# Selective-scan layer: the sums of two states' products made by accumulating DMAs, and added to y two slots later

## The chip, the core and the metric

The program runs on one core of one Trainium2 chip. The metric is the device time of the whole program in microseconds. The kernel before took 4594.26 us, the median of three runs (4590.93, 4594.26 and 4594.27). One more execution was recorded by the profiler; all rows below are from that one. Its first to its last instruction span 4588.9 us.

## The reference, cut to what matters

Input x has 4 sequences of 4096 positions with 512 features. A modulated layer norm is followed by a selective scan over 16 states, a gate and an output projection, then a second modulated norm and a small feed-forward part. The part that matters here is the scan and the sum over its states:

```
def step(h, inp):
    xt, dtt, bt, ct = inp
    dA = jnp.exp(A[None] * dtt[..., None])
    dB = dtt[..., None] * bt[:, None, :]
    h = dA * h + dB * xt[..., None]
    y = jnp.sum(h * ct[:, None, :], axis=-1)
    return (h, y)
...
y = y + D[None, None, :] * x_ssm
y = y * z
y = y @ w_out.T + b_out
```

Everything is float32. For each feature and position there are 16 products h * C, one for each state, and y is their sum.

## The kernel before, in words

**Chunks and units.** The 4 x 4096 positions are cut into 32 chunks of 512. Features lie on the 128 partitions in KD = 4 blocks. A unit is one state n of one block j: a tile of 128 partitions by 512 positions. A chunk has U = 64 units, numbered i = 4 n + j. The program is one long software pipeline: while chunk s is scanned, the projections of the next chunk f = s + 1 are made, and the output of chunk b = s - 1 and the feed-forward part of chunk c = s - 2 are finished. Each engine has its own loop over the 64 slots of a step and runs its instructions strictly in the order written; the table `ORDER` sets at which slot each piece of dense work stands.

**One unit on its way.** ScalarE makes the decay (L829) and dt * x * B (L839). TensorE transposes the latter into one of two banks of `b_ps` (`turn_v`, L453), four 128 x 128 transposes to a unit. VectorE scans (L1127) from that bank and the decay into one of 6 places of `hs`. GpSimd, called POOL in the profile, multiplies by the broadcast C row (`product`, L364) into one of PR_RING = 9 places of `pr`. TensorE adds the product to `y_ps` by four accumulating transposes (`add_unit`, L530).

**Held states.** For the states in HELD = (0, 6, 8, 13) TensorE adds nothing. When the product of the next state (1, 7, 9, 14; `summed`) is there, POOL adds the held product, which lies four units back, to it (`add_products`, L375), and TensorE adds that sum alone. So TensorE transposes 48 units of a chunk instead of 64, and POOL makes 16 sums. A unit's `add_unit` stands LAG = 4 slots after it; near the end of a chunk some stand earlier, and the last three fall in the first two slots of the next step.

**What else stands in POOL's row.** After the product (and the sum) of a slot, POOL does what is due there: the skip term (L369, slots 8 to 11), the step size dt of the next chunk for block m (`step_size`: dt by L402 at slots 42, 45, 48, 51 and u = dt * x by L410 one slot later), the gate of the present chunk (`gate`, L415) with its last block at slot 6 of the next step, and the residual additions (L384, L389).

**Who waits for POOL.** `turn_u` on TensorE transposes u of the next chunk (`dense<-ident,xn`, a L453 row; u lies in the memory of `xn`). Its first call stands in slot 54 and waits until all four blocks of u are there (`u_done` equal to KD), that is for the L410 of slot 52. `take_y` on VectorE multiplies the gate into y (L1165); its fourth block waits for the last gate, and the first `add_out` on TensorE (L566, slot 9) waits for that. `turn_v` for unit i + 1 waits for the scan of unit i - 1.

Of the kernel before, what the change touches and what calls it, by code (L numbers as in the profile page):

```python
def build_program(nc, ap, B, L, D, N, M, INNER):
# [5 lines left out]
    ALU = mybir.AluOpType  # L7
# [16 lines left out]

    HELD = (0, 6, 8, 13)
    RELU_RING = 3


# [35 lines left out]
    def summed(n):  # L64
        return n - 1 in HELD

    def sums(i):

        return sum(summed(r // KD) for r in range(i + 1))

    def added(i):

        return sum(r // KD not in HELD for r in range(i + 1))

    def slot(*part):
        return int(BEGIN[".".join(str(n) for n in part)] * U / TOTAL)
# [8 lines left out]
    with ctx:  # L85
# [15 lines left out]
        ident = sb("ident", [P, P])  # L101
# [48 lines left out]
        pr = work[:, at_pr:].rearrange("p (r t) -> p r t", r=PR_RING)  # L150
# [15 lines left out]
        def inside(s, *group):  # L166
# [8 lines left out]

        PER = {
            "SP": dict(stored_0=Q, stored_1=Q, stored_2=Q, stored_3=Q, c_stored=Q),
            "Pool": dict(prod_done=U, skip_added=KD, sum_done=sums(U - 1), xsh_done=TB, x1_done=TB, dt_done=KD, u_done=KD, sz_done=KD),
            "PE": dict(b_made=U, y_added=added(U - 1), s_ps=1, g_used=J, yz_ps=KD, out_ps=TB, res_used=TB, pre_ps=TB, xt_ps=KD, xs_ps=KD,
                       cb_ps=1, bt_ps=1, x2_ps=KD, dt_ps=KD, z_ps=KD, ut_ps=TB),  # L180
            "ACT": dict(dec_done=U, v_done=N * TB, rel_done=J, gm_done=1, lnp_done=TB, rstdp_done=TB,
                        lnx_done=1, rstdx_done=1, ln2_done=1, rstd2_done=1, t2_done=TB, xn_done=TB,
# [9 lines left out]
        x_loaded, xb_loaded, c_loaded, wm_loaded = (  # L192
            [ctx.enter_context(nc.semaphore(f"{n}_{m}")) for m in range(count)]
            for n, count in (("x_loaded", TB), ("xb_loaded", TB), ("c_loaded", C_RING), ("wm_loaded", 6)))

        def at(name, k, n):

            return (k + FIRST) * COUNT[name] + n if k < NCH else (NCH + FIRST) * COUNT[name]

        def count_up(eng, name):  # L200
            for n, c in PER[name].items():
# [138 lines left out]
        def _(gp):  # L340
# [13 lines left out]
            def product(s, i):  # L354
                n, j = i // KD, i % KD
                if j == 0:
                    gp.wait_ge(c_loaded[(s * N + n) % C_RING], ((s * N + n) // C_RING + 1) * Q)
                gp.wait_ge(S["scan_done"], at("scan_done", s, i + 1))
                k, r = (s, i - PR_RING) if i >= PR_RING else (s - 1, U + i - PR_RING)
                if r // KD in HELD:  # L360
                    gp.wait_ge(S["sum_done"], at("sum_done", k, sums(r + KD)))
                else:
                    gp.wait_ge(S["y_added"], at("y_added", k, added(r)))
                gp.tensor_tensor(pr[:, (s * U + i) % PR_RING, :], hs[:, (s * U + i) % HS_RING, :],  # L364
                                 c_bc[:, (s * N + n) % C_RING, :], ALU.mult).then_inc(S["prod_done"], 1)
                if i in SKIP_AT:
                    gp.wait_ge(S["prod_done"], at("prod_done", s, i + 1))
                    gp.wait_ge(S["skip_done"], at("skip_done", s, j + 1))
                    gp.tensor_tensor(pr[:, (s * U + i) % PR_RING, :], pr[:, (s * U + i) % PR_RING, :],  # L369
                                     xs_t[:, j, :], ALU.add).then_inc(S["skip_added"], 1)  # L370

            def add_products(s, i):

                gp.wait_ge(S["prod_done"], at("prod_done", s, i + 1))
                gp.tensor_tensor(pr[:, (s * U + i) % PR_RING, :], pr[:, (s * U + i) % PR_RING, :],  # L375
                                 pr[:, (s * U + i - KD) % PR_RING, :], ALU.add).then_inc(S["sum_done"], 1)

            def attended(b):
                for tb in range(TB):
# [68 lines left out]
        def _(pe):  # L448
# [68 lines left out]

            def add_unit(s, i):
                j = i % KD
                if i // KD in HELD:  # L520
                    return
                if i == KD:
                    pe.wait_ge(S["y_copied"], at("y_copied", s - 1, TB))
                if summed(i // KD):
                    pe.wait_ge(S["sum_done"], at("sum_done", s, sums(i)))
                pe.wait_ge(S["prod_done"], at("prod_done", s, i + 1))
                if i in SKIP_AT:
                    pe.wait_ge(S["skip_added"], at("skip_added", s, j + 1))
                for tb in range(TB):
                    last = mm(y_ps[:, tb, j * P:(j + 1) * P], pr[:, (s * U + i) % PR_RING, tb * P:(tb + 1) * P],  # L530
                              ident[:, :], is_transpose=True, start=(i == KD), stop=(i == U - 1))
                last.then_inc(S["y_added"], 1)

            def add_g(s, c, k):
# [258 lines left out]
            def step(s, has_s, has_f, has_b, has_c):  # L793
                f, b = s + 1, s - 1
                chains = [dense(s, has_s, has_f, has_b, has_c)]
                if s == 0:
                    chains.insert(0, late_rows())
                beside = Beside(*chains)
                for i in range(U):
                    if has_s and i + 1 < U:  # L800
                        turn_v(s, i + 1)
                    beside.until(i)
                    if has_f and i + 1 == U:
                        turn_v(f, 0)
                    if has_b and i < 2:
                        for r in ((U - 3, U - 2), (U - 1,))[i]:
                            add_unit(b, r)
                    if has_s and i >= LAG + 1:
                        for r in {LAG + 1: (0, 1), LAG + 2: (2,), U - 1: (U - 5, U - 4)}.get(i, (i - LAG,)):
                            add_unit(s, r)  # L810

            steps(step)
# [210 lines left out]
        def _(dve):  # L1023
# [129 lines left out]
            def take_y(s, b, c):  # L1153
                for tb in range(TB):
                    yield 2 + tb // 2
                    dve.wait_ge(S["dec_done"], at("dec_done", b, U))
                    dve.wait_ge(S["u_done"], at("u_done", b, KD))
                    dve.wait_ge(S["y_added"], at("y_added", b, added(U - 1)))
# [160 lines left out]
```

## Time and profile before

| | before |
|---|---|
| median of 3 runs | 4594.26 us |
| span of the profiled execution | 4588.9 us |
| runs' median over that span | 5.4 us |
| TensorE (PE) busy | 4344.2 us, 95% |
| POOL busy | 4161.1 us, 91% |
| ScalarE (ACT) busy | 3817.6 us, 83% |
| VectorE (DVE) busy | 3679.8 us, 80% |
| POOL: 2048 products (L364) | 2590.8 us |
| POOL: 512 sums (L375) | 653.4 us |
| granted TensorE clock, mean | 0.991 |

The profile has no time for the profiled execution but its span; the runs' median is 5.4 us longer than that, which is what lies ahead of the first and after the last instruction. Busy time is time in which an engine executes; a TensorE that is busy need not be at its peak, since matmuls overlap and their ends are modelled. How far TensorE is ahead or behind is better read from where a group of matmuls starts and where the next one does.

### The profile page before, as it was taken

What the parts mean: (1) busy time and instruction counts of PE and PEld (TensorE: products, weight loads), DVE (VectorE), ACT (ScalarE), POOL (GpSimd) and SP (SyncE); (2) the same over time, 40 slices, a digit from 0 to 9 for tenths busy, and PEclk for the clock granted to TensorE, in tenths of its full rate; (3) what the DMA queues carried; (4) which work ended last, traced back from release to release, by engine and by line L of the source; (5) the groups of instructions that cost most, each with busy time, mean ns of one, the idle gap of its engine ahead of it and who ended that gap; (6) DMA issues with size and microseconds to landing.
All of it is one profiled execution on the core that took longest, in us unless ns stands there. A gap on an engine that the chain in (4) does not pass through costs nothing. (4 is left out here: it accounts for less than half of the span.)

```text
span 4588.9 us, 71982 instructions
## 1 busy us (share of the span) xinstructions
PE 4344.2 (95%) x22528; PEld 2805.6 (61%) x22528; DVE 3679.8 (80%) x5132; ACT 3817.6 (83%) x6371; POOL 4161.1 (91%) x3343
## 2 busy tenths in 40 slices
PE   7999999999999999999999999999999999999997
PEld 3666666666666666666666666666666666666664
DVE  3778888888887888888888888888878888888885
ACT  3788888888888888888888888888888888888885
POOL 3899999999999999999999999999999999999995
PEclk8999999999999999999999999999999999999999
DMA  3111111111111111111121111111111111111111
GB/s 129 45 43 58 58 58 45 56 51 57 60 58 48 49 59 59 58 46 54 51 62 59 59 44 56 51 57 60 54 45 54 60 61 58 47 53 51 58 49 39
DMA packets 140915, 254.79 MB, mean 56 GB/s; under 512 B 18597, under 2 KB 18597, under 8 KB 140538
## 3 DMA queue, kind: packets, MB, share of 16 engines
q1 hardware_dynamic: 140538, 250.19, 17.2%
q8 instruction: 184, 3.01, 0.3%
q14 instruction: 193, 1.58, 0.1%
HBM read 215.50 MB, written 34.63 MB: 55 GB/s over the span
## 5 line engine op out<-in xcount | busy, mean ns | idle before, releaser
L364 POOL TENSOR_TENSOR work<-work,c_bc 128x512 f32<-128x512 f32 x2048 | 2590.8, 1280 | 266.6 <-DVE work L1127 180.9
L1127 DVE TENSOR_TENSOR_SCAN work<-work,state,b_ps 128x512 f32<-128x512 f32 x1792 | 2250.5, 1273 | 351.9 <-PE b_ps L453 343.2
L839 ACT ACTIVATE work<-u_td,b_td 128x512 f32<-128x512 f32 x2048 | 1455.4, 711 | 147.5 <-PE b_ps L453 142.2
L829 ACT ACTIVATE work<-dt_t,neg_a 128x512 f32<-128x512 f32 x2048 | 1454.1, 710 | 12.5 <-DVE work L1127 12.1
L453 PE MATMUL b_ps<-ident,work 128*128 128x128 f32 x8192 | 1246.2, 275 | 67.2 <-DVE work L1127 57.0
L453 PEld LDWEIGHTS b_ps<-ident,work 128*128 128x128 f32 x8192 | 966.7, 142 | 344.5 <-issue 173.4
L530 PEld LDWEIGHTS y_ps<-ident,work 128*128 128x128 f32 x6144 | 758.4, 142 | 635.7 <-issue 586.5
L530 PE MATMUL y_ps<-ident,work 128*128 128x128 f32 x6144 | 916.2, 274 | 4.7 <-POOL work L375 3.5
L375 POOL TENSOR_TENSOR work<-work 128x512 f32<-128x512 f32 x512 | 653.4, 1276 | 40.2
L679 PE MATMUL dense<-h_t,w_in_t 128*128 128x512 f32 x1024 | 514.4, 599 | 9.2 <-DVE u_td L1210 8.9
L587 PE MATMUL dense<-w_out_t,proj 128*128 128x512 f32 x1024 | 508.6, 594 | 0.0
L645 PE MATMUL dense<-xs_t,w_dt_t 128*128 128x512 f32 x1024 | 501.2, 593 | 0.0
L616 PE MATMUL dense<-h_t,w_in_t 128*128 128x512 f32 x1024 | 497.9, 595 | 1.0 <-ACT h_t L843 1.0
L1127 DVE TENSOR_TENSOR_SCAN work<-work,b_ps 128x512 f32<-128x512 f32 x256 | 306.5, 1213 | 65.7 <-PE b_ps L453 61.8
L453 PE MATMUL dense<-ident,xn 128*128 128x128 f32 x1536 | 243.6, 283 | 76.3 <-ACT xn L899 36.9
L453 PEld LDWEIGHTS dense<-ident,xn 128*128 128x128 f32 x1536 | 181.2, 144 | 207.2 <-issue 80.8
L539 PE MATMUL dense<-tmp,w_dg 128*128 128x512 f32 x512 | 245.4, 593 | 1.8 <-ACT tmp L861 1.8
L679 PEld LDWEIGHTS dense<-h_t,w_in_t 128*128 128x128 f32 x1024 | 166.7, 190 | 111.5 <-issue 76.0
L861 ACT ACTIVATE tmp<-gm,b,w 128x512 f32<-128x512 f32 x256 | 201.7, 801 | 37.4 <-PE dense L539 24.8
L616 PEld LDWEIGHTS dense<-h_t,w_in_t 128*128 128x128 f32 x1024 | 168.4, 191 | 82.6 <-issue 82.6
L402 POOL TENSOR_TENSOR dt_t<-dt_t,tmp 128x512 f32<-128x512 f32 x128 | 163.7, 1279 | 52.0 <-ACT tmp L971 52.0
L645 PEld LDWEIGHTS dense<-xs_t,w_dt_t 128*128 128x128 f32 x1024 | 165.5, 191 | 66.9 <-issue 66.9
(115 smaller groups left out, 4523.0 us busy)
## 6 DMA issues: line engine op xcount, KB each, us to landing
c_bc<-c_d SPq DMA_DIRECT2D x512, 256.0 KB, 3.2
xn<-in_x SPq DMA_DIRECT2D x128, 256.0 KB, 5.1
x<-in_x SPq DMA_DIRECT2D x128, 256.0 KB, 4.4
out_dram<-x SPq DMA_DIRECT2D x128, 256.0 KB, 4.2
work<-in_wmod SPq DMA_DIRECT2D x2, 1024.0 KB, 6.3
w_in_t<-in_w_in_t SPq DMA_DIRECT2D x2, 1024.0 KB, 9.9
gain_shift<-par_d SPq DMA_DIRECT2D x8, 256.0 KB, 4.5
w_dt_t<-in_w_dt_t SPq DMA_DIRECT2D x1, 1024.0 KB, 11.3
```

The lines of the kernel that those rows point to most:

```text
L364: gp.tensor_tensor(pr[:, (s * U + i) % PR_RING, :], hs[:, (s * U + i) % HS_RING, :], c_bc[:, (s * N + n) % C_RING, :], ALU.mult).then_inc( ...
L375: gp.tensor_tensor(pr[:, (s * U + i) % PR_RING, :], pr[:, (s * U + i) % PR_RING, :], pr[:, (s * U + i - KD) % PR_RING, :], ALU.add).then_i ...
L453: return nc.tensor.transpose(dst, src, ident[:, :])
L530: last = mm(y_ps[:, tb, j * P:(j + 1) * P], pr[:, (s * U + i) % PR_RING, tb * P:(tb + 1) * P], ident[:, :], is_transpose=True, start=(i == ...
L539: mm(long(s, "g")[:, :], w2_dg[:, k, :], tmp[:, k % RELU_RING, :], start=(k == 0), stop=(k == J - 1)).then_inc(S["g_used"], 1)
L587: last = mm(long(s, "pre", tb)[:, :], yz_t[:, k, tb * P:(tb + 1) * P], w_out[:, k, :], start=False, stop=(k == KD - 1))
L616: last = mm(long(s, "xs", m)[:, :], w_in[:, k, m * P:(m + 1) * P], h_t[:, f % 2, k, :], start=(k == 0), stop=(k == KD - 1))
L645: last = mm(long(s, "dt", m)[:, :], w_dt[:, k, m * P:(m + 1) * P], xs_t[:, k, :], start=(k == 0), stop=(k == KD - 1))
L679: last = mm(long(s, "z", m)[:, :], w_in[:, k, D + m * P:D + (m + 1) * P], h_t[:, s % 2, k, :], start=(k == 0), stop=(k == KD - 1))
L829: A(decay[:, (s * U + i) % DEC_RING, :], dt_t[:, s % 2, j, :], ACT.Exp, scale=neg_a[:, j, n:n + 1]).then_inc(S["dec_done"], 1)
L839: A(v[:, n % V_RING, tb, :], u_td[:, tb, :], ACT.Copy, scale=b_td[:, s % 2, tb, n:n + 1]).then_inc(S["v_done"], 1)
L1127: V.tensor_tensor_scan(hs[:, (s * U + i) % HS_RING, :], decay[:, (s * U + i) % DEC_RING, :], b_ps[:, i % 2, :], state[:, i:i + 1] if s % N ...
```

## The change

The sum of a held product and the next one is no longer a POOL instruction: POOL issues a DMA that adds the held unit's tile to the other's, both in on-chip memory, one DMA for each unit (16 to a chunk). Each block j has a semaphore of its own, `sum_done[j]`, which the DMA raises by Q = 16 when it has landed. `add_unit` of a summed unit stands SUM_LAG = 2 slots later than before, six slots after its unit. The fourth held state is 11 instead of 13, so that the last four sums are made in slots 48 to 51 instead of 56 to 59. `ADDS` lists the 48 units that TensorE adds in the order of their slots; the accumulation starts and ends with its first and last one. At the end of a chunk units 61, 62 and 63 are all added in slot 1 of the next step, where 61 and 62 were in slot 0.

```
-    HELD = (0, 6, 8, 13)
+    HELD = (0, 6, 8, 11)
+    SUM_LAG = 2
...
+    def add_slot(r):
+
+        return r + LAG + SUM_LAG * summed(r // KD) - (r in (U - 4, U - 2, U - 1)) - (r == U - 1)
+
+    ADDS = sorted((r for r in range(U) if r // KD not in HELD), key=lambda r: (add_slot(r), r))
...
                 if r // KD in HELD:
-                    gp.wait_ge(S["sum_done"], at("sum_done", k, sums(r + KD)))
+                    if k >= 0:
+                        gp.wait_ge(sum_done[r % KD], k * SUMS + Q * sums(r + KD))
...
             def add_products(s, i):
 
                 gp.wait_ge(S["prod_done"], at("prod_done", s, i + 1))
-                gp.tensor_tensor(pr[:, (s * U + i) % PR_RING, :], pr[:, (s * U + i) % PR_RING, :],
-                                 pr[:, (s * U + i - KD) % PR_RING, :], ALU.add).then_inc(S["sum_done"], 1)
+                gp.dma_start(pr[:, (s * U + i) % PR_RING, :], pr[:, (s * U + i - KD) % PR_RING, :],
+                             accum_op=ALU.add).then_inc(sum_done[i % KD], Q)
...
                 if summed(i // KD):
-                    pe.wait_ge(S["sum_done"], at("sum_done", s, sums(i)))
+                    pe.wait_ge(sum_done[j], s * SUMS + Q * sums(i))
...
-                    if has_b and i < 2:
-                        for r in ((U - 3, U - 2), (U - 1,))[i]:
+                    for r in ADDS:
+                        if has_b and add_slot(r) == U + i:
                             add_unit(b, r)
-                    if has_s and i >= LAG + 1:
-                        for r in {LAG + 1: (0, 1), LAG + 2: (2,), U - 1: (U - 5, U - 4)}.get(i, (i - LAG,)):
+                    for r in ADDS:
+                        if has_s and add_slot(r) == i:
                             add_unit(s, r)
```

Line numbers of the changed kernel are 8 to 10 higher at these places: the product L364 is L374 there, the sum L375 is the DMA L385, L402 and L410 are L412 and L420, and on TensorE L453, L530, L660 and L679 are L463, L538, L668 and L687.

On POOL, slots 47 to 52 of a step before: products (L364) with dt (L402) and u (L410) of the next chunk, blocks 2 and 3, between them.

```order
L364 TENSOR_TENSOR work<-work,c_bc 128x512 x2
L402 TENSOR_TENSOR dt_t<-dt_t,tmp 128x512
L364 TENSOR_TENSOR work<-work,c_bc 128x512
L410 TENSOR_TENSOR xn<-dt_t,xs_t 128x512
L364 TENSOR_TENSOR work<-work,c_bc 128x512 x2
L402 TENSOR_TENSOR dt_t<-dt_t,tmp 128x512
L364 TENSOR_TENSOR work<-work,c_bc 128x512
L410 TENSOR_TENSOR xn<-dt_t,xs_t 128x512
```

The same place of the changed kernel, from the first of the four sums, that of unit 48:

```order
L385 DMA work<-work 128x512
L412 TENSOR_TENSOR dt_t<-dt_t,tmp 128x512
L374 TENSOR_TENSOR work<-work,c_bc 128x512
L385 DMA work<-work 128x512
L420 TENSOR_TENSOR xn<-dt_t,xs_t 128x512
L374 TENSOR_TENSOR work<-work,c_bc 128x512
L385 DMA work<-work 128x512
L374 TENSOR_TENSOR work<-work,c_bc 128x512
L385 DMA work<-work 128x512
L412 TENSOR_TENSOR dt_t<-dt_t,tmp 128x512
L374 TENSOR_TENSOR work<-work,c_bc 128x512
L420 TENSOR_TENSOR xn<-dt_t,xs_t 128x512
```

Four DMA issues now stand among these rows, all of them ahead of the L420 that completes u.

On TensorE, slots 51 to 54 before: a unit's transpose (`b_ps`), one or two z projections (L679), the addition to y (L530), and in slot 54 the first transpose of u (`dense<-ident,xn`).

```order
L453 MATMUL b_ps<-ident,work 128x128 x4
L679 MATMUL dense<-h_t,w_in_t 128x512
L530 MATMUL y_ps<-ident,work 128x128 x4
L453 MATMUL b_ps<-ident,work 128x128 x4
L660 MATMUL dense<-ident,cb_t 128x32 x4
L679 MATMUL dense<-h_t,w_in_t 128x512
L530 MATMUL y_ps<-ident,work 128x128 x4
L453 MATMUL b_ps<-ident,work 128x128 x4
L679 MATMUL dense<-h_t,w_in_t 128x512 x2
L530 MATMUL y_ps<-ident,work 128x128 x4
L453 MATMUL b_ps<-ident,work 128x128 x4
L453 MATMUL dense<-ident,xn 128x128 x4
```

The changed kernel from slot 52 to slot 55:

```order
L463 MATMUL b_ps<-ident,work 128x128 x4
L668 MATMUL dense<-ident,cb_t 128x32 x4
L687 MATMUL dense<-h_t,w_in_t 128x512
L463 MATMUL b_ps<-ident,work 128x128 x4
L687 MATMUL dense<-h_t,w_in_t 128x512 x2
L463 MATMUL b_ps<-ident,work 128x128 x4
L463 MATMUL dense<-ident,xn 128x128 x4
L538 MATMUL y_ps<-ident,work 128x128 x4
L463 MATMUL b_ps<-ident,work 128x128 x4
L687 MATMUL dense<-h_t,w_in_t 128x512 x2
L538 MATMUL y_ps<-ident,work 128x128 x4
```

The additions to y that stood in slots 48 to 53 are gone from there (six groups of four), so the transpose of u comes earlier by as much; the six stand in slots 56 to 59, which had none.

## Rows read from the trace of the kernel before

**Rows 1.** The page's head and busy time of each engine

```profile
span 4588.9 us, 71982 instructions
PE 4344.2 (95%) x22528; PEld 2805.6 (61%) x22528; DVE 3679.8 (80%) x5132; ACT 3817.6 (83%) x6371; POOL 4161.1 (91%) x3343
```

**Rows 2.** Costliest groups: line, engine, operation, count | busy, mean ns | idle before

```profile
L364 POOL TENSOR_TENSOR work<-work,c_bc 128x512 f32<-128x512 f32 x2048 | 2590.8, 1280 | 266.6 <-DVE work L1127 180.9
...
L375 POOL TENSOR_TENSOR work<-work 128x512 f32<-128x512 f32 x512 | 653.4, 1276 | 40.2
```

**Rows 3.** Waits, all engines: who waited for whom, us in total, times, longest

```profile
DVE proj L1165 <- POOL sz_t L415: 64.5, 30, 2.3
...
PE dense L566 <- DVE proj L1165: 45.2, 30, 1.5
```

**Rows 4.** Waits of TensorE alone

```profile
PE dense L453 <- POOL xn L410: 5.6, 6, 2.8
```

**Rows 5.** Busy time in slots 48 to 53 of one step, 13.55 us long

```profile
core 0: us, PE busy (x) PEld busy (x) DVE busy (x) ACT busy (x) POOL busy (x), PEclk, DMA share, GB/s
2274.35:2287.90 13.55, 13.55 (x73) 8.75 (x72) 8.62 (x11) 9.27 (x16) 13.55 (x12) 1.00 0.14 41
```

**Rows 6.** TensorE in order of time: start, length, group [idle before, releaser]

```profile
2287.45 0.60 PE L530 MATMUL y_ps<-ident,work 128*128 128x128 f32 x4
2287.89 0.60 PE L453 MATMUL b_ps<-ident,work 128*128 128x128 f32 x4
2288.41 0.63 PE L453 MATMUL dense<-ident,xn 128*128 128x128 f32 x4
2288.87 0.60 PE L530 MATMUL y_ps<-ident,work 128*128 128x128 f32 x4
2289.60 0.63 PE L453 MATMUL b_ps<-ident,work 128*128 128x128 f32 x4
...
2296.53 0.66 PE L453 MATMUL dense<-ident,xn 128*128 128x128 f32 x4 [0.65 <-DVE tmp L1225]
...
2301.36 1.13 PE L679 MATMUL dense<-h_t,w_in_t 128*128 128x512 f32 x2 [0.29 <-DVE u_td L1210]
```

**Rows 7.** POOL in order of time, the same step, slots 46 to 53

```profile
2272.85 1.27 POOL L364 TENSOR_TENSOR work<-work,c_bc 128x512 f32<-128x512 f32 x1
2274.08 1.29 POOL L410 TENSOR_TENSOR xn<-dt_t,xs_t 128x512 f32<-128x512 f32 x1
2275.32 2.51 POOL L364 TENSOR_TENSOR work<-work,c_bc 128x512 f32<-128x512 f32 x2
2277.79 1.26 POOL L402 TENSOR_TENSOR dt_t<-dt_t,tmp 128x512 f32<-128x512 f32 x1
...
2286.42 1.26 POOL L410 TENSOR_TENSOR xn<-dt_t,xs_t 128x512 f32<-128x512 f32 x1
```

**Rows 8.** VectorE in order of time: the scan of unit 46

```profile
2270.31 1.27 DVE L1127 TENSOR_TENSOR_SCAN work<-work,state,b_ps 128x512 f32<-128x512 f32 x1
```

**Rows 9.** POOL in order of time at the start of that step, slots 4 to 6

```profile
2177.61 1.28 POOL L364 TENSOR_TENSOR work<-work,c_bc 128x512 f32<-128x512 f32 x1 [2.08 <-DVE work L1127]
2180.03 1.28 POOL L364 TENSOR_TENSOR work<-work,c_bc 128x512 f32<-128x512 f32 x1 [1.14 <-issue]
2181.38 1.28 POOL L375 TENSOR_TENSOR work<-work 128x512 f32<-128x512 f32 x1
2182.62 1.29 POOL L364 TENSOR_TENSOR work<-work,c_bc 128x512 f32<-128x512 f32 x1
...
2187.82 1.27 POOL L415 TENSOR_TENSOR sz_t<-sz_t,tmp 128x512 f32<-128x512 f32 x1
```

**Rows 10.** VectorE at the same place

```profile
2189.22 0.69 DVE L1165 TENSOR_TENSOR proj<-sz_t,dense 128x512 f32<-128x512 f32 x1 [2.13 <-POOL sz_t L415]
```

**Rows 11.** TensorE at the same place

```profile
2187.52 0.60 PE L530 MATMUL y_ps<-ident,work 128*128 128x128 f32 x4
...
2190.06 1.10 PE L566 MATMUL dense<-wout_g,gm 128*128 128x512 f32 x2 [1.50 <-DVE proj L1165]
...
2194.06 0.60 PE L530 MATMUL y_ps<-ident,work 128*128 128x128 f32 x4
```

**Rows 12.** SyncE's issues of the C rows' DMAs, 256 KB each: duration ns min/median/max

```profile
L298 SPq DMA_DIRECT2D c_bc<-c_d x512: 319/320/430, 65.0 to 4502.0; - x171
...
DMA to landing us min/median/max: 3.0/3.2/4.8
```

**Rows 13.** DMA issues by line: KB each, median us from issue to landing

```profile
xn<-in_x SPq DMA_DIRECT2D x128, 256.0 KB, 5.1
```

More of the change, by code:

```diff
@@ L67, in sums, with added @@
     def sums(i):
-        return sum(summed(r // KD) for r in range(i + 1))
-    def added(i):
-        return sum(r // KD not in HELD for r in range(i + 1))
+        return sum(summed(n) for n in range(i // KD + 1))
+    def add_slot(r):
+        return r + LAG + SUM_LAG * summed(r // KD) - (r in (U - 4, U - 2, U - 1)) - (r == U - 1)
+    ADDS = sorted((r for r in range(U) if r // KD not in HELD), key=lambda r: (add_slot(r), r))
+    def added(r):
+        return ADDS.index(r) + 1
     def slot(*part):
@@ L177, in build_program @@
             "SP": dict(stored_0=Q, stored_1=Q, stored_2=Q, stored_3=Q, c_stored=Q),
-            "Pool": dict(prod_done=U, skip_added=KD, sum_done=sums(U - 1), xsh_done=TB, x1_done=TB, dt_done=KD, u_done=KD, sz_done=KD),
-            "PE": dict(b_made=U, y_added=added(U - 1), s_ps=1, g_used=J, yz_ps=KD, out_ps=TB, res_used=TB, pre_ps=TB, xt_ps=KD, xs_ps=KD,
+            "Pool": dict(prod_done=U, skip_added=KD, xsh_done=TB, x1_done=TB, dt_done=KD, u_done=KD, sz_done=KD),
+            "PE": dict(b_made=U, y_added=len(ADDS), s_ps=1, g_used=J, yz_ps=KD, out_ps=TB, res_used=TB, pre_ps=TB, xt_ps=KD, xs_ps=KD,
                        cb_ps=1, bt_ps=1, x2_ps=KD, dt_ps=KD, z_ps=KD, ut_ps=TB),
@@ L191, in build_program @@
         S = {n: ctx.enter_context(nc.semaphore(n)) for n in once + list(COUNT)}
-        x_loaded, xb_loaded, c_loaded, wm_loaded = (
+        x_loaded, xb_loaded, c_loaded, wm_loaded, sum_done = (
             [ctx.enter_context(nc.semaphore(f"{n}_{m}")) for m in range(count)]
-            for n, count in (("x_loaded", TB), ("xb_loaded", TB), ("c_loaded", C_RING), ("wm_loaded", 6)))
+            for n, count in (("x_loaded", TB), ("xb_loaded", TB), ("c_loaded", C_RING), ("wm_loaded", 6), ("sum_done", KD)))
         def at(name, k, n):
             return (k + FIRST) * COUNT[name] + n if k < NCH else (NCH + FIRST) * COUNT[name]
+        SUMS = Q * len(HELD)
         def count_up(eng, name):
@@ L519, in add_unit @@
                 j = i % KD
-                if i // KD in HELD:
-                    return
-                if i == KD:
+                if i == ADDS[0]:
                     pe.wait_ge(S["y_copied"], at("y_copied", s - 1, TB))
                 if summed(i // KD):
-                    pe.wait_ge(S["sum_done"], at("sum_done", s, sums(i)))
+                    pe.wait_ge(sum_done[j], s * SUMS + Q * sums(i))
                 pe.wait_ge(S["prod_done"], at("prod_done", s, i + 1))
@@ L530, in add_unit @@
                     last = mm(y_ps[:, tb, j * P:(j + 1) * P], pr[:, (s * U + i) % PR_RING, tb * P:(tb + 1) * P],
-                              ident[:, :], is_transpose=True, start=(i == KD), stop=(i == U - 1))
+                              ident[:, :], is_transpose=True, start=(i == ADDS[0]), stop=(i == ADDS[-1]))
                 last.then_inc(S["y_added"], 1)
@@ L1157, in take_y @@
                     dve.wait_ge(S["u_done"], at("u_done", b, KD))
-                    dve.wait_ge(S["y_added"], at("y_added", b, added(U - 1)))
+                    dve.wait_ge(S["y_added"], at("y_added", b, len(ADDS)))
                     V.tensor_copy(y_sb[:, b % 2, tb, :], y_ps[:, tb, :]).then_inc(S["y_copied"], 1)
```

## The prediction

> **What bounds the kernel now.** I read the page's busy times first. TensorE is busy 95% of the span and POOL 91%, the others 80 to 83% [rows 1], so either of two engines may set the pace. The groups show what the change takes off POOL: 512 sums of 1.276 us, 653 us in all [rows 2]. Read as a share, that is a seventh of the span; the question is what of it stands on the path.
>
> The second view is the busy time of one stretch. In slots 48 to 53 TensorE and POOL are both busy for the whole 13.55 us at a granted clock of 1.00, while VectorE has 8.62 us of work [rows 5]. In order of time TensorE's groups there follow each other at their issue distance, 0.44 us for four transposes (2287.45 to 2287.89) [rows 6]. So in the second half of a step TensorE sets the pace, and POOL is only just not late: its backlog of products does no harm as long as no TensorE instruction needs its end.
>
> The third view, the waits, says where POOL does reach the others. VectorE waits 64.5 us in 30 steps for the last gate, and TensorE's L566 45.2 us in 30 for VectorE right behind it [rows 3]: about 1.5 us a step at its start. And TensorE has waited for u (L410) 6 times, 5.6 us in all [rows 4]. That row is small, but it shows that the second contact exists and has little slack. The two places decide this change.
>
> **The start of a step.** In the step shown POOL makes product 4 at 2180.03, its sum, product 5 at 2182.62, two more sums, and the gate at 2187.82 [rows 9]. VectorE stands 2.13 us until the gate is there [rows 10], and TensorE's L566 starts at 2190.06 after 1.50 us of waiting for VectorE [rows 11]. A summed product takes 2.59 us from start to start (2180.03 to 2182.62), an unsummed one 1.24 (2274.08 to 2275.32) [rows 7, 9]; so a sum costs POOL 1.35 us, 0.07 of it waiting for its own product. A DMA that occupies POOL for d would cost d + 0.07, and three of them stand ahead of the gate: it comes 3 x (1.28 - d) earlier. At most about 2 us of that is of use: VectorE waits no longer than 2.13, and TensorE, which loses an addition to y in slot 8 (0.44 us, the one at 2187.52), would stand 1.50 + 0.44. The additions of slots 8 and 9 come back in slots 12 and 13. There they fill waits that I count as unchanged.
>
> **The end of a step, where the cost is.** Two edits meet here. Six additions leave slots 48 to 53, so TensorE reaches the first transpose of u not at 2288.41 but 6 x 0.44 = 2.64 us earlier, at 2285.77 [rows 6]. VectorE can follow that pace: 8.62 us of work in the 10.9 that are left [rows 5]. Meanwhile four sums enter POOL's row between product 48 and the last L410, a stretch in which POOL had no gap. Before, that stretch ran from 2276.56 (the second of the two products that start at 2275.32) to 2287.68 (2286.42 + 1.26), 11.12 us [rows 7]. With four DMAs it takes 11.12 + 4 x (d + 0.07).
>
> It may begin earlier. The eight sums in slots 28 to 39 save 8 x (1.28 - d), 2.2 us for d = 1, but product 46 can't start ahead of its scan's end at 2271.58 [rows 8] (2270.31 + 1.27); at 2271.66 it would be 1.19 us earlier than it was, 2272.85, and product 48 follows three steps of 1.24 later, at 2275.38. Then u is complete at 2275.38 + 11.12 + 0.28 + 4d = 2286.78 + 4d. TensorE is there at 2285.77 and waits 1.0 + 4d. It executes strictly in order, so behind that wait stand the next units' transposes, and VectorE's scans behind those. The six additions left out are still owed in slots 56 to 59, so none of the wait is got back by them; they only fill the waits that follow: 0.29 us before the b_ps group at 2289.60 (2288.87 + 0.44 = 2289.31), 0.65 at 2296.53 and 0.29 at 2301.36 [rows 6], together 1.23. VectorE, which has done two scans more by then, is no later. The end of a step gets longer by 4d - 0.2.
>
> **What d is.** No row shows a DMA issued by POOL. The nearest below is SyncE's issue of a DMA of the same 256 KB, 0.32 us [rows 12]; less than that isn't to be expected of an instruction that must give out the same 128 rows. The nearest on POOL is its own pass over 128 rows, 1.28 us [rows 2]. The far end above is that POOL stands until the data has landed, 3.2 to 5.1 us [rows 12, 13]. POOL has to work out the transfer itself, so I take a value nearer to POOL's row than to SyncE's, three quarters of the way from 0.32 to 1.28: 1.0 us.
>
> The Trainium skill, DMA: Bandwidth & Descriptors, section Latency and other measured facts, gives about 1 us to the first byte for a DMA that GpSimd issues, against 600 ns from the others, and lays it to the GpSimd cores writing the descriptors. Taken as d, an estimate, it gives the same sum; no row here shows it. The same page, section Anatomy of one DMA, calls descriptor generation small and gives most of the delay to the landing; by that d would be near the lower end, the first rival below.
>
> **The sum.** For d = 1.0: the end of a step costs 1.0 + 4.0 - 1.23 = 3.8 us, its start gives back 3 x 0.28 = 0.84: 3.0 us a step. 31 steps have both places, 92 us. The profiled execution's span is 4588.9; 5.4 us lie around it by the runs' median of 4594.3. So 4594.3 + 92 = 4686.
>
> **Edits that I cost at nothing.** The later additions and the landing: the sum of unit 4, issued at about 2181.4, is added where unit 6 was, at 2194.06 [rows 9, 11], 12.7 us later; a 256 KB transfer lands in 3.2 to 5.1 us [rows 12, 13]. The ring: product i + 5 reuses the place of the unit that was added to product i; four products and the issue, 4 x 1.24 + d = 6 us, lie between. If landing took longer than that, POOL would stand for the difference. TensorE's work is the same 48 units. Units 61 and 62 moved from slot 0 to slot 1: unit 63's place, for which the copies of y wait, is the same. SyncE issues what it did. The transfers (512 of 256 KB, 134 MB) meet queues that are seldom full; if not, they land later, which is the third rival.
>
> **Rivals.**
> *Cheap issue: faster.* If POOL only hands the DMA on, d = 0.32 as on SyncE, the end of a step costs 4 x 0.32 - 0.2 = 1.1 and the start gives its full 2.0: -0.9 a step, 29 us, 4565. For it speaks that a DMA moves no data through POOL; against it that on POOL's row every listed operation of this width costs 1.28. The point of decision is d = 0.58, where 4d - 0.2 equals 3 x (1.28 - d).
> *Issue as long as the sum or longer.* At d = 1.28 nothing is saved: the gate comes when it did, product 46 is not earlier (1.19), and the end costs 1.0 + 1.19 + 5.1 - 1.23 = 6.1 us a step: 4783. Each further 0.1 us adds over 1 us a step. For it: every transfer of this kind names three rows (two read, one written); against: nothing in the trace.
> *Late landing.* An addition reads its target as well; at twice 5.1 us the ring's 6 us are overrun by 4, in slots 35 to 40, where POOL has some slack, and TensorE stands for sums four times a step: some 6 us a step on top, 4870. Against: the queues' light load.
> *The wait for u doesn't form,* because TensorE doesn't get ahead, or POOL runs earlier than I count: then only the start counts, 0.84 to 2 us a step, 4568 to 4532.
>
> **How the numbers follow.** My forecast, d from 0.75 to 1.1, has 0.36 and by itself spans 4631 (1.2 us a step) to 4707 (3.6). Cheap issue has 0.24, no wait 0.06, d around 0.58 with less than 9 us either way 0.12, an issue of over 1.1 us 0.18, late landing 0.04. A change under 0.2% (9 us) can't be told from none. So faster 0.30, same 0.12, slower 0.58. The range, 4560 to 4785, leaves out the larger gains below and the long issues and late landings above.
>
> **What would show it.** The profile after should have DMA issues on POOL of about 1 us (the first thing to read); TensorE's transpose of u waiting for POOL's L420 in some 31 steps, about 5 us each; the wait for the gate shorter by less than 1 us; POOL's busy time, without its issues, down by 653 us, and the span longer all the same. It is wrong if issues take under 0.6 us or if the wait for u stays a rare one.

## The result: 4.9% slower, and the profile after

The changed kernel takes 4815.9 us (median of 4 runs, 4815.3 to 4816.9), the kernel before on the same chip 4592.9: ratio 1.0486, 95% interval 1.0471 to 1.0501. That is 223 us, 7.0 us in each of the 32 steps. The forecast was 4686 within 4560 to 4785. The sign is right, the size is more than twice the forecast and outside the range.

The page of the kernel after, the head and three of its groups (line, engine, operation, count | busy, mean ns | idle before), answers to [rows 1, 2]:

```profile
span 4813.9 us, 71981 instructions
...
PE 4412.0 (92%) x22528; PEld 2866.4 (60%) x22528; DVE 3677.8 (76%) x5132; ACT 3822.5 (79%) x6371; POOL 3989.7 (83%) x3343
...
L374 POOL TENSOR_TENSOR work<-work,c_bc 128x512 f32<-128x512 f32 x2048 | 2778.5, 1414 | 534.4 <-DVE work L1135 418.2
...
L385 POOL DMA_DIRECT2D work<-work x512 | 449.1, 877 | 163.5 <-POOL work L374 148.3
...
work<-work POOLq DMA_DIRECT2D x512, 256.0 KB, 3.3
```

The last line is of the list of DMA issues: 3.3 us from issue to landing. An issue occupies POOL for 877 ns by its record. But its true price is larger, and two things show it. POOL is idle 148.3 us before the issues, waiting for its own product. And the mean product lasts 1414 ns, where it was 1280 [rows 2]. By the busy share POOL is relieved, 83% for 91%; by the waits it is not. The waits of the kernel after (who waited for whom, us in total, times, longest) answer to [rows 3, 4]:

```profile
PE dense L463 <- POOL xn L420: 190.3, 32, 7.1
...
DVE proj L1173 <- POOL sz_t L425: 57.3, 30, 3.1
...
PE dense L574 <- DVE proj L1173: 51.0, 30, 2.9
```

TensorE's wait for u was 5.6 us in 6 places and is 190.3 us in 32, 5.9 us a step. The wait for the gate has hardly changed: 57.3 us for 64.5 on VectorE, 51.0 for 45.2 on TensorE.

POOL in order of time at the end of a step, answering to [rows 7] (product 48 is the second of the two at 2385.29, so it starts 1.24 later, at 2386.53):

```profile
2385.29 2.75 POOL L374 TENSOR_TENSOR work<-work,c_bc 128x512 f32<-128x512 f32 x2
2388.34 0.88 POOL L385 DMA_DIRECT2D work<-work  x1 [0.30 <-POOL work L374]
2388.95 1.57 POOL L412 TENSOR_TENSOR dt_t<-dt_t,tmp 128x512 f32<-128x512 f32 x1
2390.19 1.56 POOL L374 TENSOR_TENSOR work<-work,c_bc 128x512 f32<-128x512 f32 x1
2392.04 0.88 POOL L385 DMA_DIRECT2D work<-work  x1 [0.30 <-POOL work L374]
2392.65 1.58 POOL L420 TENSOR_TENSOR xn<-dt_t,xs_t 128x512 f32<-128x512 f32 x1
...
2401.28 1.55 POOL L420 TENSOR_TENSOR xn<-dt_t,xs_t 128x512 f32<-128x512 f32 x1
```

This is what an issue costs in a row without gaps. The product ahead of it must have ended: 0.30 us. The next instruction starts 0.61 us after the issue starts (2388.34 to 2388.95). And the instructions behind an issue last 1.57 us, not 1.28; they still start 1.24 apart, but whoever waits for the end of one, the next issue above all, waits 0.3 us longer. From 2390.19 to 2392.65 the product and its issue take 2.46 us, where a product alone takes 1.24: this DMA costs POOL 1.22. Over the whole trace the price is 1.24 us where the product ahead is itself one of the longer ones (the middle value of 435 issues), and 0.94 where that product has its ordinary length (of 64). The addition it replaces cost 1.35.

From product 48 to the end of the last L420 (2401.28 + 1.55 = 2402.83) this step has 16.30 us, where it had 11.12: four DMAs at 1.30, the last piece's longer record included.

TensorE at the same place, answering to [rows 6]:

```profile
2396.70 0.60 PE L463 MATMUL b_ps<-ident,work 128*128 128x128 f32 x4
2402.88 1.12 PE L463 MATMUL dense<-ident,xn 128*128 128x128 f32 x4 [5.58 <-POOL xn L420]
2403.79 1.06 PE L538 MATMUL y_ps<-ident,work 128*128 128x128 f32 x4
2404.65 1.06 PE L463 MATMUL b_ps<-ident,work 128*128 128x128 f32 x4
2405.50 3.56 PE L687 MATMUL dense<-h_t,w_in_t 128*128 128x512 f32 x4
2408.89 0.60 PE L538 MATMUL y_ps<-ident,work 128*128 128x128 f32 x4
```

It is ready for u at 2397.14 (2396.70 + 0.44) and starts at 2402.88, 5.74 us later and only 0.05 us after POOL's L420 ends. What follows is new: four transposes take 0.85 to 0.91 us from start to start, where they took 0.44, and the four matmuls of 512 columns 3.39. The busy time of the same stretches (columns as in [rows 5], the granted clock stands behind POOL's) says why:

```profile
2395.00:2402.00 7.00, 2.30 (x10) 1.05 (x8) 3.83 (x5) 6.39 (x12) 6.41 (x7) 1.00 0.60 114
2402.00:2406.00 4.00, 3.12 (x13) 2.96 (x14) 0.85 (x2) 1.50 (x3) 4.00 (x4) 0.50 0.03 5
2406.00:2410.00 4.00, 4.00 (x15) 2.01 (x14) 1.17 (x2) 0.72 (x1) 1.76 (x2) 0.64 0.19 66
2410.00:2420.00 10.00, 10.00 (x63) 7.35 (x62) 8.22 (x12) 5.80 (x10) 6.33 (x5) 1.00 0.04 12
```

Behind the wait TensorE's granted clock is 0.50, the lower of its two levels (1.2 GHz for 2.4). From 2402.88 to 2408.89 are 6.01 us; at the full clock the same matmuls take 3 x 0.44 + 1.72 = 3.04. So in this row the wait costs 5.74 us and the slow clock behind it another 2.97. This step is one of the dearer ones: over the 31 steps that have the place, the same stretch takes 4.41 to 6.03 us, 5.38 in the mean, so the slow clock costs 2.3 us a step. The Trainium skill, TensorE: Matmul & The Clock Gate, section Part 1: The HAM clock gate (the "warmup" mystery), ties this clock to how busy the engine has lately been; these rows agree.

The start of the same step, answering to [rows 9]:

```profile
2291.17 1.27 POOL L374 TENSOR_TENSOR work<-work,c_bc 128x512 f32<-128x512 f32 x1 [1.15 <-issue]
2292.74 0.89 POOL L385 DMA_DIRECT2D work<-work  x1 [0.30 <-POOL work L374]
2293.35 1.59 POOL L374 TENSOR_TENSOR work<-work,c_bc 128x512 f32<-128x512 f32 x1
...
2298.34 1.57 POOL L425 TENSOR_TENSOR sz_t<-sz_t,tmp 128x512 f32<-128x512 f32 x1
```

From product 4 to the end of the gate 8.74 us pass (2298.34 + 1.57 - 2291.17), before 9.06 (2187.82 + 1.27 - 2180.03): 0.32 us earlier. The first issue adds 0.94 us (2291.17 to 2293.35, less 1.24), the other two 2.51 together, where three additions added 4.05; of these 0.6 us the gate's own longer record takes back 0.3.

### The profile page after: what moved, and what is told of

Read it like the earlier page. It is cut to its first block and busy times, and to the rows that moved or that the text cites. A ratio compares the mean times of both kernels' runs of the same rounds, so it can differ in the third digit from the quotient of the medians.

```text
span 4813.9 us, 71981 instructions
## 1 busy us (share of the span) xinstructions
PE 4412.0 (92%) x22528; PEld 2866.4 (60%) x22528; DVE 3677.8 (76%) x5132; ACT 3822.5 (79%) x6371; POOL 3989.7 (83%) x3343
## 3 DMA queue, kind: packets, MB, share of 16 engines
q0 software_dynamic: 73728, 134.25, 16.1%
## 5 line engine op out<-in xcount | busy, mean ns | idle before, releaser
L374 POOL TENSOR_TENSOR work<-work,c_bc 128x512 f32<-128x512 f32 x2048 | 2778.5, 1414 | 534.4 <-DVE work L1135 418.2
L463 PE MATMUL b_ps<-ident,work 128*128 128x128 f32 x8192 | 1262.1, 278 | 64.9 <-DVE work L1135 57.3
L463 PEld LDWEIGHTS b_ps<-ident,work 128*128 128x128 f32 x8192 | 992.5, 143 | 467.5 <-issue 296.6
L538 PEld LDWEIGHTS y_ps<-ident,work 128*128 128x128 f32 x6144 | 758.8, 144 | 508.2 <-issue 486.1
L538 PE MATMUL y_ps<-ident,work 128*128 128x128 f32 x6144 | 895.0, 277 | 4.3 <-DMA work<-work 3.6
L385 POOL DMA_DIRECT2D work<-work x512 | 449.1, 877 | 163.5 <-POOL work L374 148.3
L687 PE MATMUL dense<-h_t,w_in_t 128*128 128x512 f32 x1024 | 543.9, 631 | 1.1 <-DVE u_td L1218 1.1
L624 PE MATMUL dense<-h_t,w_in_t 128*128 128x512 f32 x1024 | 497.8, 595 | 1.0 <-ACT h_t L851 1.0
L463 PE MATMUL dense<-ident,xn 128*128 128x128 f32 x1536 | 257.9, 295 | 238.4 <-POOL xn L420 190.3
L463 PEld LDWEIGHTS dense<-ident,xn 128*128 128x128 f32 x1536 | 189.5, 150 | 373.0 <-POOL xn L420 197.8
L1218 DVE COPY u_td<-dense 128x512 f32<-128x512 f32 x128 | 88.2, 689 | 243.7 <-PE dense L463 243.7
L687 PEld LDWEIGHTS dense<-h_t,w_in_t 128*128 128x128 f32 x1024 | 183.8, 206 | 107.0 <-issue 104.4
L412 POOL TENSOR_TENSOR dt_t<-dt_t,tmp 128x512 f32<-128x512 f32 x128 | 197.9, 1546 | 52.1 <-ACT tmp L979 52.1
L984 ACT ACTIVATE tmp<-tmp 128x512 f32<-128x512 f32 x128 | 79.8, 624 | 180.0 <-DVE tmp L1233 180.0
```

The source lines that it names most:

```text
L385: gp.dma_start(pr[:, (s * U + i) % PR_RING, :], pr[:, (s * U + i - KD) % PR_RING, :], accum_op=ALU.add).then_inc(sum_done[i % KD], Q)
L463: return nc.tensor.transpose(dst, src, ident[:, :])
L624: last = mm(long(s, "xs", m)[:, :], w_in[:, k, m * P:(m + 1) * P], h_t[:, f % 2, k, :], start=(k == 0), stop=(k == KD - 1))
L687: last = mm(long(s, "z", m)[:, :], w_in[:, k, D + m * P:D + (m + 1) * P], h_t[:, s % 2, k, :], start=(k == 0), stop=(k == KD - 1))
```

## The experiments

Theory A: POOL's price of an issue, four times between product 48 and u, makes u late while TensorE comes earlier; the wait and the clock behind it are the time. Theory B: the additions' later places cost the time by themselves. Theory C: the DMAs' traffic or landings cost it. The ratios are to runs of the kernel before on the same chip; the names are those of the headings below.

| run | median us | ratio, 95% interval |
|---|---|---|
| no_sum | 4506.3 | 0.9811 (0.9796 to 0.9825) |
| h13 | 4606.4 | 1.0030 (1.0018 to 1.0042) |
| pool_h11 | 4840.5 | 1.0540 (1.0522 to 1.0558) |
| fill | 4747.2 | 1.0335 (1.0319 to 1.0350) |
| rows32 | 4782.4 | 1.0421 (1.0404 to 1.0439) |
| pair_h13 | 4579.9 | 0.9971 (0.9960 to 0.9982) |
| pair_h11 | 4607.3 | 1.0030 (1.0019 to 1.0042) |
| pair_6 | 4665.3 | 1.0156 (1.0141 to 1.0171) |
| pair_h13w | 4552.2 | 0.9912 (0.9896 to 0.9929) |
| pair_h11w | 4623.4 | 1.0069 (1.0054 to 1.0084) |

### no_sum: no sums at all, the additions at their new places

```diff
-                if r // KD in HELD:
-                    if k >= 0:
-                        gp.wait_ge(sum_done[r % KD], k * SUMS + Q * sums(r + KD))
-                else:
+                if r // KD not in HELD:
...
-                        if summed(i // KD):
-                            add_products(s, i)
```

> The changed kernel without its 512 accumulating DMAs; the held products are left out of y (that part of the computation is missing), every slot stays where the change put it. Theory A: the loss of 7.2 us a step is POOL's occupation by four issues between product 48 and the end of u (4 x 1.29 us by the trace after), which TensorE waits out in slot 54, and half clock behind that wait. Then the wait for u shrinks from 5.7 us to under 1, the granted clock stays at 1.00 there, the gate comes about 2 us earlier, and the time is 4520 to 4580. Theory B: the new places of the additions to y alone break TensorE's row; then it stays above 4700. Theory C: the DMAs' traffic slows the other engines; it too says about 4590 here, and is told apart by the next run.

It took 4506.3 us. Its wait for u, from the waits of TensorE:

```profile
PE dense L458 <- POOL xn L417: 15.1, 32, 2.8
```

With the six additions as late as in the changed kernel and nothing in POOL's row in place of the sums, TensorE waits 0.5 us a step. So B falls: the places alone don't cost the time. The gain is larger than expected. TensorE's wait for VectorE at the gate is gone from the list as well; slot 10, which holds it, takes 2.3 us where it took 4.3 before.

### h13: the DMAs, at the places that the additions had

```diff
-    HELD = (0, 6, 8, 11)
+    HELD = (0, 6, 8, 13)
```

> The changed kernel with the fourth held state back at 13: the same 512 DMAs, but the last four of a step stand in slots 56 to 59, behind the end of u, and the six additions don't leave slots 48 to 53. Theory A: the wait for u is gone in nearly all steps, the clock stays up, and the time is 4580 to 4630. Theory C (traffic of the DMAs): it stays near 4800, since the same bytes move. Theory B (places of additions): near 4600 as well.

It took 4606.4 us. All 512 DMAs are there, and TensorE waits for u once, 2.8 us. The traffic (C) costs at most the 0.3% by which this run is slower than the kernel before. Where neither stands ahead of u, the DMAs in place of the additions, with the two slots' delay of the additions to y, are worth nothing. TensorE's wait at the gate stays:

```profile
PE dense L574 <- DVE proj L1173: 51.6, 30, 2.9
```

### pool_h11: the new places, with additions on POOL

```diff
...
-                gp.dma_start(pr[:, (s * U + i) % PR_RING, :], pr[:, (s * U + i - KD) % PR_RING, :],
-                             accum_op=ALU.add).then_inc(sum_done[i % KD], Q)
+                gp.tensor_tensor(pr[:, (s * U + i) % PR_RING, :], pr[:, (s * U + i) % PR_RING, :],
+                                 pr[:, (s * U + i - KD) % PR_RING, :], ALU.add).then_inc(sum_done[i % KD], 1)
...
```

> The changed kernel's slots and held states, with the sums made by POOL additions again: no DMA. Theory A: an addition costs POOL 1.35 us and the eight sums ahead save nothing, so product 48 is not earlier (2276.56 on the axis of the trace before), u is complete at 2276.56 + 11.12 + 4 x 1.36 = 2293.1 against TensorE's 2285.8: a wait of about 7.3 us, with the half clock behind it about 8.5 to 9 us a step: 4850 to 4890, slower than the changed kernel. Theory C: back to about 4600. Theory B: like the changed kernel, about 4816.

It took 4840.5 us, a little under the expected range, and slower than the changed kernel, as A has it:

```profile
PE dense L463 <- POOL xn L420: 225.3, 32, 8.5
```

The wait for u is 7.0 us a step with additions, 5.9 with DMAs. No DMA makes the sums here and the wait is longer still, so C falls for the new places too. With h13 this separates the two halves of the change: at the new places the DMA in place of the addition gives 25 us (4840.5 - 4815.9), and the move of the last held state from 13 to 11 costs 210 us with DMAs (4815.9 - 4606.4). With additions the move and the two slots' delay together cost 248 (4840.5 - 4592.4, the kernel before on that chip); no run has that delay alone.

### fill: the wait for u filled with matmuls that nobody reads

```diff
+                    pe.wait_ge(S["zmax_done"], at("zmax_done", s, 2))
+                    for _ in range(6 if s >= 0 else 0):
+                        mm(to[:, :], w_in[:, 0, D:D + P], h_t[:, s % 2, 0, :], start=True, stop=True)
                     pe.wait_ge(S["u_done"], at("u_done", f, KD))
-                    pe.wait_ge(S["zmax_done"], at("zmax_done", s, 2))
```

> The changed kernel with six matmuls of 128x512 put ahead of TensorE's wait for u, whose results are overwritten: TensorE works through most of the 5.7 us instead of standing. Theory A with the clock as a term of its own: the wait's end doesn't move, the granted clock behind it stays at 1.00 instead of 0.50, and 2.5 to 2.9 us a step come back: 4725 to 4745. If the clock is not what makes the groups behind the wait longer: 4810 to 4825.

It took 4747.2 us, 69 us less than the changed kernel: 2.15 us a step, somewhat under the expected 2.5 to 2.9. TensorE in order of time, the fillers first (each of the six is recorded as two matmuls):

```profile
2361.05 5.42 PE L697 MATMUL dense<-h_t,w_in_t 128*128 128x512 f32 x12 [0.27 <-DVE tmp L1235]
2366.43 0.66 PE L463 MATMUL dense<-ident,xn 128*128 128x128 f32 x4
...
2367.79 1.88 PE L687 MATMUL dense<-h_t,w_in_t 128*128 128x512 f32 x4
2369.51 0.60 PE L538 MATMUL y_ps<-ident,work 128*128 128x128 f32 x4
```

The groups that took 6.01 us behind the wait take 3.08 here (2366.43 to 2369.51), though u comes as late as before: from product 48 to the last L420's end POOL takes 16.35 us in this step, where it took 16.30. So the slow clock is a term of its own, and not a sign of something else that is late. Over the 31 steps these groups take 3.08 or 3.09 us each time, in the changed kernel 5.38 in the mean; of these 2.3 us a step 2.15 reach the end.

### rows32: the same issues over a quarter of the rows

```diff
-                gp.dma_start(pr[:, (s * U + i) % PR_RING, :], pr[:, (s * U + i - KD) % PR_RING, :],
+                gp.dma_start(pr[0:32, (s * U + i) % PR_RING, :], pr[0:32, (s * U + i - KD) % PR_RING, :],
```

> The changed kernel with its 512 DMAs each over 32 of the 128 rows (64 KB in place of 256 KB): the sum of the other 96 rows is left out. Theory R (GpSimd's price of an issue goes with the rows that it has to describe): the issue's record falls from 0.88 us to 0.25 to 0.5, a DMA costs GpSimd some 0.6 to 0.9 us in place of 1.25, TensorE waits for u 2.5 to 4.5 us a step in place of 5.7, and the time is 4680 to 4770 us. Theory F (the price is one per issue, whatever it moves): record 0.88 us, the time as the changed kernel, 4800 to 4830 us; only the landing is shorter than 3.3 us.

GpSimd's DMA queue (packets, MB), the group and its landing, from the page:

```profile
q0 software_dynamic: 24576, 33.59, 6.3%
...
L385 POOL DMA_DIRECT2D work<-work x512 | 410.8, 802 | 162.7 <-POOL work L374 148.8
...
work<-work POOLq DMA_DIRECT2D x512, 64.0 KB, 2.5
```

A quarter of the rows and bytes takes 802 ns in place of 877. From product 48 to the end of u the middle one of the 31 steps takes 15.79 us in place of 16.28, so an issue costs 1.17 us there in place of 1.29. The price is nearly one per issue, which is theory F with a small part that goes with the rows or bytes; the time, 4782.4 us, lies between the two ranges, 18 us under F's and 12 over R's. The wait for u is 169.0 us, where it was 190.3.

### pair_h13 and pair_h11: one DMA for two units

The edit against the changed kernel; pair_h13 also has HELD = (0, 6, 8, 13).

```diff
-    V_RING, DEC_RING, HS_RING, PR_RING, C_RING = 2, 6, 6, 9, 3
+    V_RING, DEC_RING, HS_RING, PR_RING, C_RING = 2, 6, 6, 10, 3
...
-        w_cb = sb("w_cb_t", [P, KD, P])
+        w_cb = sb("w_cb_t", [P, KD, 2 * N])
...
+                to, of = ((s * U + r) % PR_RING for r in (i - 1, i - 1 - KD))
+                gp.dma_start(pr[:, to:to + 2, :], pr[:, of:of + 2, :], accum_op=ALU.add
+                             ).then_inc(sum_done[i % KD // 2], Q)
...
-                        if summed(i // KD):
+                        if summed(i // KD) and i % 2:
...
```

> The states held back as before the change (0, 6, 8, 13), the sums by DMA, but one DMA of 512 KB for two units: eight DMAs a step in place of sixteen. Theory A (a DMA costs GpSimd about 1.25 us per issue, whatever it moves): ahead of the gate's operation stands one issue in place of three, so the gate is about 2 us earlier than in the run with single DMAs at these places (139.7 us a step), 137.5 to 138.3 us a step, 4530 to 4570 us in all. Theory D (the cost goes with the bytes or rows, so that one DMA of two units costs what two of one unit cost): 139 to 140 us a step, 4590 to 4620 us. The landing may grow from 3.3 us; by neither theory does anything wait for it more than 0.5 us a step.

> The changed places (states 0, 6, 8 and 11 held back), one DMA of 512 KB for two units. Theory A: between the 48th product and the last piece of u stand two issues (2.5 us) in place of four (5.0), so TensorE waits for u 3 to 3.5 us a step in place of 5.7, and stands at the lower clock for less: 140.5 to 143 us a step, 4630 to 4730 us. Theory D (cost by bytes): as the changed kernel, 4790 to 4830 us.

The queue, the group of issues and their landing (pair_h13's page; pair_h11's group differs by 0.1 us):

```profile
q0 software_dynamic: 36864, 134.23, 15.4%
...
L386 POOL DMA_DIRECT2D work<-work x256 | 225.1, 879 | 82.1 <-POOL work L374 74.3
...
work<-work POOLq DMA_DIRECT2D x256, 512.0 KB, 5.6
```

Twice the bytes, and the issue's record is 879 ns. Theory D falls. The queue's counts say what is the same: 144 packets to a DMA here (36864 over 256) as in the changed kernel (73728 over 512), since the two units lie side by side in each row; the DMA of rows32 has 48. So it is rows32 that varies the number of packets: a third of them takes 0.08 us less. The Trainium skill, DMA: Bandwidth & Descriptors, section Anatomy of one DMA, says that many descriptors can be emitted before the incremental cost shows; rows32 agrees. The same section counts setup as small beside the landing. By these rows it is not negligible: POOL pays 0.88 us of record for every issue, against a landing of 3.3.

pair_h11 took 4607.3 us, 209 us less than the changed kernel and below A's range. Two parts were in it. The wait for u is 66.2 us in 32 places, 2.1 us a step, where I had expected 3 to 3.5; POOL's two issues are not cheaper, 13.61 us from product 48 to the end of u in the middle one of 31 steps, 1.24 each over the 11.12. And the gate, with one issue ahead of it for three, is no longer waited for at all, which I had not counted for this run. That second part I had counted for pair_h13, at 4530 to 4570 us; it came out at 4579.9, out of range. The slots of the two traces show where the rest stayed: slot 10, which held the wait for the gate, fell from 4.3 to 2.3 us, but slots 49 to 51 had become 0.27, 0.27 and 0.32 us longer. They hold the matmuls whose weights my edit had cut to 32 columns to make room for the tenth buffer.

### pair_h13w and pair_h11w: that side effect taken away

Against the two runs above:

```diff
-        w_cb = sb("w_cb_t", [P, KD, 2 * N])
+        w_cb = sb("w_cb_t", [P, (KD - 1) * 2 * N + P])
...
-                last = mm(long(s, "cb")[0:2 * N, :], w_cb[:, k, :], xs_t[:, k, :], start=(k == 0), stop=(k == KD - 1))
+                last = mm(long(s, "cb")[:, :], w_cb[:, k * 2 * N:k * 2 * N + P], xs_t[:, k, :], start=(k == 0), stop=(k == KD - 1))
```

> The run with one DMA for two units and the old places (0, 6, 8, 13), with one side effect of its edit taken away: there the weights of the product that makes B and C were cut to 32 columns to find room for the tenth product buffer, and the slots 49, 50 and 51 that hold this product's matmuls became 0.27, 0.27 and 0.32 us longer (0.86 us a step). Here the matmul reads 128 columns again, out of a packed tile (the rows of its result that nobody reads hold other columns). Theory A: nothing waits at the end of the step with these places, so the whole 0.86 us a step comes back: 138.0 us a step, 4545 to 4560 us. Rival (the narrow weights were not the cause, or the time is taken back elsewhere): 4575 to 4585 us.

> The same repair in the run with one DMA for two units and the changed places (0, 6, 8, 11). Theory A: there the end of the step is set by GpSimd (u behind two issues), so the 0.84 us that TensorE saves in the slots 49 to 51 only brings it earlier to the wait for u: the wait grows from 2.1 to about 2.9 us a step, and the time stays at 4600 to 4612 us. Rival (TensorE's own work sets the step): 0.84 us less a step, 4575 to 4585 us.

pair_h13w took 4552.2 us, as A had it: 28 us less, which is the 0.86 us a step. It is the fastest of the kernels that make the sums, 0.9% under the kernel before.

The same 0.84 us less work on TensorE made pair_h11w slower: 4623.4 us. TensorE around u in pair_h11, and then in pair_h11w:

```profile
2295.75 0.60 PE L464 MATMUL b_ps<-ident,work 128*128 128x128 f32 x4
2298.37 1.07 PE L464 MATMUL dense<-ident,xn 128*128 128x128 f32 x4 [2.02 <-POOL xn L421]
2299.24 1.06 PE L539 MATMUL y_ps<-ident,work 128*128 128x128 f32 x4
2300.09 1.06 PE L464 MATMUL b_ps<-ident,work 128*128 128x128 f32 x4
2300.94 2.35 PE L688 MATMUL dense<-h_t,w_in_t 128*128 128x512 f32 x4
```

```profile
2300.99 0.60 PE L464 MATMUL b_ps<-ident,work 128*128 128x128 f32 x4
2304.47 0.66 PE L464 MATMUL dense<-ident,xn 128*128 128x128 f32 x4 [2.88 <-POOL xn L421]
2304.96 0.83 PE L539 MATMUL y_ps<-ident,work 128*128 128x128 f32 x4
2305.58 1.06 PE L464 MATMUL b_ps<-ident,work 128*128 128x128 f32 x4
2306.44 2.96 PE L688 MATMUL dense<-h_t,w_in_t 128*128 128x512 f32 x4
```

The wait grew from 2.02 to 2.88 us: TensorE only came sooner to a u that is due when POOL is done. That was A's expectation, 4600 to 4612. The 11 us above it are the clock, but these two rows don't show it: from the first transpose of u to the group behind the four matmuls both take the same, 4.75 and 4.77 us, only the slow part begins later in the second. The 31 steps show it. Either the clock stays up behind the wait and the stretch takes 3.08 us, in 12 steps of pair_h11 and in 5 of pair_h11w, or it falls and the stretch takes up to 4.77 and 6.03. The mean rises from 4.11 to 4.58 us, the wait by 0.83, and TensorE's 0.84 less ahead of it are lost: 0.46 us a step, 14 of the 16 us between the runs. The mean granted clock, 0.980 for 0.984, says the same.

### pair_6: six states held back

```diff
-    HELD = (0, 6, 8, 13)
+    HELD = (0, 2, 4, 6, 8, 13)
```

> Six states held back (0, 2, 4, 6, 8, 13), one DMA of 512 KB for two units: twelve DMAs a step, and TensorE transposes 40 units where it transposed 48. Theory A: TensorE is given back 1.75 us for each further state, 3.5 us a step; GpSimd carries four issues more (5 us), but all of them in the middle of the step: 134 to 137 us a step, 4420 to 4530 us. Theory D (cost by bytes): GpSimd carries twelve DMAs at 2.5 us, 30 us a step where the additions cost 21.8, becomes late in the middle of the step, and the time is 4580 us or more.

This is pair_h13's edit with this line on top. It took 4665.3 us, against both theories: D asked for issues of 2.5 us, and their records are 0.88 as above; A's sum left something out. TensorE's waits show what:

```profile
PE b_ps L464 <- DVE work L1136: 141.7, 168, 5.7
PE dense L464 <- ACT xn L908: 60.4, 30, 2.2
```

and VectorE's a wait that is 0.6 us in pair_h13:

```profile
DVE norm L1153 <- POOL x L400: 47.1, 31, 3.9
```

In slots 15 to 24, states 3 to 6, POOL also makes the residual additions of the chunk before (L395, L400). By these waits the four further issues make those late, so norm and xn are late, and TensorE's transposes and VectorE's scans behind them; no run takes that apart. I had taken those slots as free because no wait stood there before. It is the same mistake as with u, at another contact.

## Why the prediction was wrong

**What was right.** TensorE came to u 2.6 us earlier (slots 49 to 54 are 0.43 us shorter each), found it late in all 32 steps, and the four issues ahead of u set the length of the wait. no_sum, pool_h11 and pair_h11 show this from three sides. Of the waits that the owed additions were to fill, 1.23 us a step, two are listed in TensorE's waits before:

```profile
PE dense L453 <- DVE tmp L1225: 19.9, 31, 0.6
...
PE dense L679 <- DVE u_td L1210: 8.9, 28, 1.1
```

They went nearly whole: the first is gone from the list after, the second fell to 1.1 us. Nothing waited long for a landing (3.6 us in all for the sums), the ring held, and late landing was rightly the smallest rival. One sign came out otherwise: POOL's busy time without its issues is down by 483 us (4161.1 to 3678.4), not 653, since the records behind an issue are longer. The prediction's 5.4 us around the span are 1.8 by each run's time beside its own span (4815.72 and 4813.9 here); the sum doesn't depend on them.

**The step that failed most: the end of a step was a wait alone.** "The end of a step costs 1.0 + 4.0 - 1.23 = 3.8 us" has no term for what TensorE does behind the wait. The granted clock of 0.50 costs 2.97 us in the row, 2.3 in the mean of the steps and, by fill, 2.15 us a step in the time: 69 of the 223 us. [Rows 5] showed 1.00 where TensorE had worked without a gap; the prediction took it for the whole end of the step, though the sum itself brought a gap of 5 us into it.

**d was too small.** "three quarters of the way from 0.32 to 1.28: 1.0 us". The record is 0.88, and the price in a row without gaps 1.24, where the forecast's d + 0.07 is 1.07: the 0.07 of waiting for its own product was carried over from the addition, where the issue has 0.30, and what the instructions behind it take longer was not foreseen. With the longer record of the last L420 shared out, the row has 1.30 in place of 1.07 four times, so 0.9 us more between product 48 and u. Product 48 came 10.61 us ahead of TensorE's being ready (2386.53 to 2397.14), where the forecast had 10.39 (2275.38 to 2285.77). 5.0 + 0.9 - 0.2 = 5.7, the wait of the row. The Trainium skill's 1 us (DMA: Bandwidth & Descriptors, section Latency and other measured facts), which the prediction set beside d, is near the issue's record and 0.24 us short of the price.

**The start gave nothing.** "its start gives back 3 x 0.28 = 0.84": the gate is 0.32 us earlier, and TensorE lost slot 8's addition, 0.44 us, ahead of it. Its wait there grew from 45.2 to 51.0 us. The mechanism is real: with one issue ahead of the gate in place of three, pair_h13 and pair_h11 lose the wait whole, 2.0 us a step.

Together, per step: the wait for u +5.8 ((190.3 - 5.6) / 32), the clock +2.2, the gate +0.2, listed waits filled -0.9: 7.3, against 7.0 measured. The forecast's rival "issue as long as the sum or longer" was nearest in d, and its 4783 lacked the clock too.

Left open: why the instructions behind an issue last 0.3 us longer on POOL. No run here takes it apart. Open too is why in four of the 31 steps one of the four issues starts 1.0 to 1.6 us late; nothing that it waits for shows.

## What to carry to other kernels

Price an edit at the contact where one engine first waits for another, not by the engine's busy share: here POOL's share fell by 8 points and its last piece came 5 us later. A DMA issued by POOL in place of an addition relieves it by 0.1 us of 1.35; what pays is fewer issues, one for two units that lie side by side in each row, away from the instruction that others wait for. A stand of TensorE has a second price behind it in the clock, and work saved on TensorE ahead of such a stand can cost time.

## What the runs showed of the hardware

- An accumulating DMA issued by POOL: 802, 877 and 879 ns of record for 64, 256 and 512 KB (48, 144 and 144 packets), and 2.5, 3.3 and 5.6 us to landing.
- The POOL instructions behind such an issue last 1.53 to 1.60 us in place of 1.28, several in a row, while their starts stay 1.24 apart.
- Behind a stand of 2.02 us on TensorE the granted clock is already down for a time in the step of pair_h11 shown (four transposes in 0.87 us for 0.44), but not in every step: behind waits of 1.9 to 2.8 us it fell in 19 of that run's 31 steps and stayed up in 12. Behind the wait at the gate, 1.61 us in the step of the kernel after, it stays at 1.00, the first number behind POOL's in the second view here:

```profile
2300.87 1.10 PE L574 MATMUL dense<-wout_g,gm 128*128 128x512 f32 x2 [1.61 <-DVE proj L1173]
```

```profile
2300.80:2302.80 2.00, 1.93 (x4) 0.68 (x4) 1.97 (x4) 1.68 (x3) 1.70 (x3) 1.00 0.18 61
```
- Matmuls with 32 columns of weights among matmuls with 128 cost 0.86 us a step more than the same matmuls with 128 columns (pair_h13 against pair_h13w).
